# A graph-attention kernel with its matmul rows set on a wider pitch, and two small loads moved late

## The reference

```python
def _L0_gnn_ref(h, adj, W, a):
    Wh = h @ W
    e = (Wh @ a1)[:, None] + (Wh @ a2)[None, :]
    e = jnp.where(e > 0, e, ALPHA * e)
    e = jnp.where(adj > 0, e, MASK_VAL)
    attention = jax.nn.softmax(e, axis=1)
    return jax.nn.elu(attention @ Wh)
def _L1_gnn_ref(x, adj, weight, bias):
    deg = jnp.sum(a, axis=1, keepdims=True)
    x1 = a @ x / deg
    return jnp.concatenate([x1, x], axis=1) @ weight + bias
x = _layernorm(x + _L0_gnn_ref(x, adj, L0_gnn_W, L0_gnn_a), axis=-1)
x = _layernorm(x + _L1_gnn_ref(x, adj, L1_gnn_weight, L1_gnn_bias), axis=-1)
```

## Time and profile before

| | before |
|---|---|
| median of three runs | 1530.68 us |
| lowest and highest | 1529.59, 1532.32 us |
| span of the profiled execution, first to last instruction | 1530.0 us |
| PE busy | 1480.1 us, 97% |
| PE weight loads (PEld) busy | 1295.9 us, 85% |
| DVE busy | 980.3 us, 64% |
| ACT busy | 970.7 us, 63% |
| POOL busy | 118.0 us, 8% |
| chain that ended last, share of PE | 93% |
| mean granted clock of TensorE | 0.988 |

### The profile page before, as it was taken

How to read it: one execution, slowest core, us unless ns; L and a number is a source line. 1 busy time by engine, 2 the same in 40 slices (tenths; PEclk the granted TensorE clock), 3 DMA queues, 4 the chain that set the end, 5 groups by cost and what they waited for, 6 DMA issues and landing times.

```text
span 1530.0 us, 38618 instructions
## 1 busy us (share of the span) xinstructions
PE 1480.1 (97%) x14086; PEld 1295.9 (85%) x14086; DVE 980.3 (64%) x2781; ACT 970.7 (63%) x2384; POOL 118.0 (8%) x199
## 2 busy tenths in 40 slices
PE   7489999999999999999999999989999999999997
PEld 6378888888888888888888888878888888888886
DVE  7887877787777787777777777654343434444343
ACT  3799999999999999999999999921000000001000
POOL 1001100110010010010001000000000000000000
PEclk9699999999999999999999999999999999999999
DMA  9967998788778868878877880050000000000000
GB/s 172 114 71 81 118 103 95 81 90 95 86 85 96 91 80 96 93 81 92 93 85 87 95 92 22 12 137 15 17 17 17 17 17 17 17 17 14 17 17 17
DMA packets 99722, 101.70 MB, mean 66 GB/s; under 512 B 4704, under 2 KB 66912, under 8 KB 99680
## 3 DMA queue, kind: packets, MB, share of 16 engines
q0 software_dynamic: 33792, 67.11, 44.1%
q1 hardware_dynamic: 65888, 34.03, 9.2%
HBM read 289.77 MB, written 12.68 MB: 198 GB/s over the span
## 4 chain that ended last, share of the span: by engine, by line
PE 93%; DVE 2%; ACT 2%; DMA 1%; issue 1%; SPq 0%; POOL 0%; DVEq 0%; POOLq 0%
PE acc L621 59%; PE acc L696 30%; PE turn_ps L720 2%; ACT level_ring L424 1%; PE pack_ps L580 1%; PE turn_ps L710 1%; DVE words L768 1%; DVE wh_top L776 1%; DMA s_and_t<-words 1%; DMA s_row<-s_and_t 0%; ACT factors L472 0%; DMA factors<-in_x 0%; PE acc L569 0%; DVE words L825 0%; PE turn_ps L559 0%
## 5 line engine op out<-in xcount | busy, mean ns | idle before, releaser
L424 ACT ACTIVATE level_ring<-s_row,cols 128x256 fp8e4<-128x256 f32 x2048 | 832.5, 497 | 0.0
L621 PE MATMUL acc<-factors,edge_ring 128*128 128x258 f16 x4096 | 550.3, 273 | 21.7 <-DVE edge_ring L902 20.5
L621 PE MATMUL acc<-factors,level_ring 128*128 128x258 f16 x4096 | 550.1, 273 | 0.0
L696 PE MATMUL acc<-factors,adj_space 128*128 128x258 f16 x4096 | 469.6, 273 | 4.6 <-issue 4.6
L696 PEld LDWEIGHTS acc<-factors,adj_space 128*128 128x128 fp8e4 x4096 | 399.6, 98 | 63.6 <-issue 4.8
L621 PEld LDWEIGHTS acc<-factors,edge_ring 128*128 128x128 fp8e4 x4096 | 363.7, 97 | 75.6 <-issue 22.5
L621 PEld LDWEIGHTS acc<-factors,level_ring 128*128 128x128 fp8e4 x4096 | 363.8, 97 | 53.6 <-issue 0.3
L895 DVE TENSOR_TENSOR level_ring<-level_ring,edge_ring 128x1024 uint16<-128x1024 uint16 x256 | 174.3, 691 | 190.6 <-ACT level_ring L424 180.1
L522 ACT ACTIVATE part_sums<-acc 128x258 f32<-128x258 f32 x32 | 12.4, 387 | 297.7 <-PE acc L696 297.7
L580 PE MATMUL pack_ps<-pack_w,adj_space 128*128 128x32 bf16 x960 | 170.1, 177 | 0.0
L902 DVE TENSOR_TENSOR edge_ring<-edge_ring,level_ring 128x1024 uint16<-128x1024 uint16 x256 | 166.5, 682 | 0.0
(11 more groups left out here) (95 smaller groups left out, 709.9 us busy)
## 6 DMA issues: line engine op xcount, KB each, us to landing
adj_space<-in_adj POOLq DMA_DIRECT2D x64, 1024.0 KB, 16.8
x_parts<-parts SPq DMA_DIRECT2D x32, 129.0 KB, 4.6
factors<-x_parts SPq DMA_DIRECT2D x8, 516.0 KB, 6.4
factors<-in_x SPq DMA_DIRECT2D x8, 512.0 KB, 7.3
s_row<-s_and_t SPq DMA_DIRECT2D x32, 128.0 KB, 3.6
rows_x<-in_x SPq DMA_DIRECT2D x32, 128.0 KB, 2.1
x_rows<-rows_y SPq DMA_DIRECT2D x32, 128.0 KB, 9.8
rows_x<-x_rows SPq DMA_DIRECT2D x32, 128.0 KB, 2.1
```

Source lines behind the costliest of these rows:

```text
L424: a = act.activation(level_bytes[:, h % MASK_SLOTS, j, :], s_row[:, slot, :], ACT.Relu, bias=t_big[:, h * HALF + j:h * HALF + j + 1], scal ...
L621: m = pe.matmul(acc[a][:, 0:ROW], mask, factors[:, neg, jj, :], start=(jj == 0), stop=(jj == NJ - 1))
L696: m = pe.matmul(acc[b][:, 0:ROW], ring_1_bytes[:, c, j, b * P:(b + 1) * P], factors[:, 0, jj, :], start=(jj == 0), stop=(jj == NJ - 1))
```

## The change

Rows of `factors` are 264 elements (528 bytes) apart; the six elements behind each row are never written or read. The tile grows by 1536 bytes a partition. As much is freed: `w1_sb` and `bias_row` have no tiles of their own any more and lie in slot 0 of `edge_ring`, into which they are loaded once the softmax stage is over. SP issues these two loads behind the first load of rows of the mean stage; PE waits for the weights in the first `project` and DVE for the bias in the first `add_bias`.

```diff
+    PITCH = ROW + (-ROW) % 8
...
-        factors = sb("factors", [P, 2, NJ, ROW], F16)
+        factors = sb("factors", [P, 2, NJ, PITCH], F16)
...
-        bias_row = sb("bias_row", [P, F], F32)
-        w1_sb = sb("w1_sb", [P, 2, F], F32)
...
+        late = edge_ring[:, 0, :, :].rearrange("p j r -> p (j r)").bitcast(F32)
+        w1_sb = late[:, 0:2 * F].rearrange("p (k o) -> p k o", k=2)
+        bias_row = late[:, 2 * F:3 * F]
...
-            sp.dma_start(w1_sb[:, :, :], w1.rearrange("(k f) o -> f k o", k=2)).then_inc(w1_in, 16)
-            sp.dma_start(bias_row[:, :], b1.partition_broadcast(P)).then_inc(bias_in, 16)
             sp.wait_ge(s_turn_ok, 1)
...
-                sp.dma_start(factors[:, 0, HALF * k:HALF * (k + 1), :], parts_tiles[:, HALF * k:HALF * (k + 1), :])\
+                sp.dma_start(factors[:, 0, HALF * k:HALF * (k + 1), 0:ROW], parts_tiles[:, HALF * k:HALF * (k + 1), :])\
                     .then_inc(parts_in[k], 16)
...
             rows_1(0)
+            sp.dma_start(w1_sb, w1.rearrange("(k f) o -> f k o", k=2)).then_inc(w1_in, 16)
+            sp.dma_start(bias_row, b1.partition_broadcast(P)).then_inc(bias_in, 16)
             with sp.Fori(1, NG) as g:
...
-                        m = pe.matmul(acc[a][:, 0:ROW], mask, factors[:, neg, jj, :],
+                        m = pe.matmul(acc[a][:, 0:ROW], mask, factors[:, neg, jj, 0:ROW],
                                       start=(jj == 0), stop=(jj == NJ - 1))
...
-                        m = pe.matmul(acc[b][:, 0:ROW], ring_1_bytes[:, c, j, b * P:(b + 1) * P], factors[:, 0, jj, :],
+                        m = pe.matmul(acc[b][:, 0:ROW], ring_1_bytes[:, c, j, b * P:(b + 1) * P], factors[:, 0, jj, 0:ROW],
                                       start=(jj == 0), stop=(jj == NJ - 1))
...
                 pe.wait_ge(turned1_ok, g + 1)
-                if not first:
+                if first:
+                    pe.wait_ge(w1_in, 16)
+                else:
                     pe.wait_ge(y1_ok, g)
...
-            pe.wait_ge(w1_in, 16)
             group_1(0, first=True)
...
                 dve.wait_ge(rows1_in, 16 * (g + 1))
-                if not first:
+                if first:
+                    dve.wait_ge(bias_in, 16)
+                else:
                     dve.wait_ge(y_out, 16 * g)
...
-            dve.wait_ge(bias_in, 16)
             dve.wait_ge(x1_out, 16 * NG)
```

More of the change, by code:

```diff
@@ L315, in _ @@
                 sp.wait_ge(w_stored, 32 * (NJ + 1))
-                sp.dma_start(factors[:, 0, :, :], parts_tiles).then_inc(w_parts_in, 16)
+                sp.dma_start(factors[:, 0, :, 0:ROW], parts_tiles).then_inc(w_parts_in, 16)
             def rows_1(g):
```

## The result

The changed kernel takes 1512.45 us (median of 4 runs, 1511.19 to 1513.46) against 1531.5 us (4 runs, 1529.59 to 1534.62): a ratio of 0.9878, interval 0.9866 to 0.9891, a gain of 19.05 us where 29.4 had been forecast. The direction and the place were right. The time lies above the range.

A forecast was written before the change was run, and what follows sets the result against it. PE's stream was taken to bound the kernel (busy 97% of the span). Gains of 18.8 us (softmax stage) and 10.6 us (mean stage) summed to 29.4 us, a span of 1500.6 us, forecast 1501.3 us; range 1498.5 to 1509 us.

The forecast's parts named there:

- My reading: Matmuls on `factors`: each pays 3.44 ns when its row begins in the line where the previous one's row ended.
- The packing part: Softmax stage, large matmuls alternating with small ones: one packing `multiply` takes 3.91 us instead of 3.96.
- The late loads and their waits: Start of the mean stage: weights and bias arrive with 10 and 3.5 us of cover, cost 0.
- The loads removed at the start: SP's queue at the program's start: two loads fewer, taken as 0, bounds 0 to 2.2 us of gain.
- The loads of `factors`: Loads before the mean stage (line 290): taken as 0, a loss of up to 1.8 us, once, if the last lands late.
- The writes to `factors`: ACT and DVE instructions writing `factors` with the new step: taken as 0, 0.7 us either way if they felt the pitch.
- ACT's slack: Softmax stage: of ACT's 1.05 us wait for PE's sums in a group, 0.44 us stay, so cost 0.
- The projection: Its 256 matmuls, reading weights from another place: taken as 0, a gain of 0.6 us if they came down to 109 ns.
- Rival 1: Matmuls on `factors`: a row ending inside a line holds up the next matmul, so slower, 1539.2 us; chance 0.04.
- Rival 2: Whole kernel: no effect, as the pattern of four has another source or line crossings alone count, 1530.7 us; chance 0.04.
- the reading by lines touched: Rows of `factors`: 33 lines touched at either pitch, so by crossings alone the time stays at 1530.7 us.
- Rival 3: Softmax stage: ACT's loop limits the gain, 1510.7 us with half of it, 1520.1 us with none; chance 0.07.

The follow-up runs named there:

- the 520 set: Changed kernel with rows 532 bytes apart in the first set and 520 in the second, whose odd rows share a line with even ones: 1515.06 us (one run).

## Why the prediction was wrong

**The cause was right, and is shown.** A matmul whose row begins in the line where the previous one's row ended pays for it. The kernel that changes only the reading order gets the whole gain, the late loads alone get none, and shifted rows keep it.

**The step that failed** is the last sentence of "My reading": "With a pitch of 528 = 33 x 16 bytes neither happens again", taken together with its price of 3.44 ns. That none shares a line held. That each of them then falls to 109.2 ns did not: I took the shortest step in the trace for the price without the fault. But a stream of 258 columns with no shared line steps 110.0 ns = (258 + 6)/2.4. In the kernel before the 109.2 ns stood only beside a step of 112.6 or a small matmul, and the neighbours were early where another was late. The fault has to be priced against the stream without it, on the average: 111.75 - 110.0 = 1.75 ns a matmul, not 111.75 - 109.2 = 2.6.

**The mis-sized terms.** There are 6,016 plain matmuls in groups 1 to 31 and 4,096 in the mean stage: 10,112 x 0.83 = 8.4 us too much. The small packing matmul steps 26.75 ns and not 26: 960 x 0.7 = 0.7 us. The sum less these is 29.4 - 9.1 = 20.3 us, and the groups' own differences make 20.2. The packing part escaped the error, since its large matmuls stand beside small ones and do step 109.2 ns, so its forecast of 3.91 us was nearly met (3.92).

**A warning set aside.** The two levels that I read, 109.2 and 112.6 ns, lie on both sides of 110.0. The Trainium skill, "TensorE: Matmul & The Clock Gate", section Back-to-back issue gap, gives N/2.4 + 2.5 ns, as the gap of an isolated matmul at the full clock, and says that a stream with weight loads departs from it. I wrote that the records disagree with it. The streams of these runs, each matmul with a weight load of its own, agree with it on average to about 0.1 ns at 254, 256, 258, 260 and 264 columns wherever no line was shared. As an estimate by its 110.0 ns, the sum would have come out at 10,112 x 1.75 = 17.7 us for the plain matmuls and, with 247.8 ns for two large and a small one before and 220.0 + 26 after, 960 x 1.8 = 1.7 us for the packing: 19.4 us, so 1511.3 us.

**The terms of nothing** held. The late loads and their waits: nothing waits, with more cover than forecast. The loads removed at the start: with the late loads alone the time is the same within 0.15%. The loads of `factors`: the last is issued at 1010.36 us and lands 5.2 us later, PE reads its first row at 1018.71 us, and no step of the first group is long there. Before, that row was read at 1032.05 us, not near 1031.6 as I had it, which changes no term. The writes to `factors`: ACT and DVE are as busy as before. ACT's slack: 0.64 us are left in a group, and would have been 0.44 with the forecast group. The projection: 0.89 us for eight in the chain, as before.

**The rivals.** Rival 1 (the row's end decides) fell in the change itself: after it, every row ends 4 bytes into a line, and 96 plain matmuls take 10.56 us, not 10.81; the 520 set says the same. Rival 2 fell with the gain, and with it the reading by lines touched: rows of 33 lines step 110.0 ns at one pitch and 111.75 on average at the other. Rival 3 fell by ACT's wait. **The range** failed with the sum: its high end held the costs of waits and half of rival 3, but no doubt about the 109.2 ns, the one number that all the gain rested on. A bound from the same rows would have been to let the long steps fall only part of the way.

## What to carry to other kernels

Where two levels of a repeated step show a fault, its price is measured against a stream that has no fault anywhere, not against the short steps beside it; without such a stream in the trace, the mean and the short step bound the gain from two sides. Where successive matmuls read rows that meet inside a 16-byte line, take the rows in an order in which neighbours don't follow each other, or space them apart: the order alone gave the same time here, with no memory and no change to the writers. Where PE is full, count columns: each two cost 0.83 ns of every step, and 257 cost as much as 258.

## What the runs showed of the hardware

- A matmul with 258 moving columns whose row begins in the line where the previous row ended steps 112.6 ns under pitches of 516 and 520 bytes and 114.2 under 524. On the stream's mean, a sharing matmul costs 2.3, 1.96 and 1.84 ns over the step of a stream without sharing.
- Without sharing, the mean step of a plain stream is the columns plus six cycles at 2.4 GHz: 108.3, 109.2, 110.0, 110.8 and 112.5 ns for 254, 256, 258, 260 and 264 columns, with a weight load of its own for each; 257 columns step like 258.
- Neighbours of a late step can be early (109.2 ns for 258 columns), also without any shared line, as at pitch 532, where 110.0, 111.7, 109.1 and 109.2 ns repeat and make 110.0. Under 516 bytes read evens first, steps of 112.3 ns stand among such of 109.2 and make 110.1.
- The price was seen at the full clock alone. At the start of the mean stage, PE having stood idle for 4.6 us in the kernel before and 4.9 us in the changed one, the granted clock is 0.50 (1.2 GHz). There matmuls step 215 ns on average in both, over 15 and 25 steps, which is 258/1.2: with shared lines as without.

Open: why the late step is 112.6 ns at two pitches and 114.2 at a third, and what lets the neighbours of a late or a small matmul run two cycles short. No run here separates these.
